# A four-layer transformer kernel: second layer's experts on 23 sorted token spans instead of 72 gated ones

## The reference, cut to what matters

```
logits = x @ Wg                                  # 4096 tokens, 8 experts
probs = softmax(logits)
vals, idx = top_k(probs, 2)
weights = vals / (sum(vals) + 1e-9)
cw = zeros(T, E).at[arange(T)[:, None], idx].set(weights)
act = silu(einsum('th,ehf->tef', x, W1) + b1)     # F = 512
y = einsum('tef,efh->teh', act, W2) + b2
out = einsum('te,teh->th', cw, y)
out = out + 0.1 * (silu(x @ Ws1 + bs1) @ Ws2 + bs2)
```

## Time and profile before

| | us |
|---|---|
| median of 3 runs | 4922.42 |
| the profiled execution, whole | 4929.4 |
| its span, first to last instruction | 4927.6 |
| TensorE busy | 4247.0 (86%) |
| VectorE busy | 3604.9 (73%) |
| ScalarE busy | 3188.9 (65%) |
| GpSimd busy | 2235.6 (45%) |
| granted TensorE clock, mean | 0.942 of full |

### The profile page before, as it was taken

The page is one execution under the profiler, slowest core; times in us unless marked ns, Lnnn a source line. Parts: engine busy times, 40 slices in busy tenths (PEclk is TensorE's granted clock), DMA queues, the critical chain, the costliest instruction groups (busy, mean ns, idle before and its releaser), DMA issues. The chain is left out here.

```text
span 4927.6 us, 91117 instructions
## 1 busy us (share of the span) xinstructions
PE 4247.0 (86%) x35369; PEld 2321.4 (47%) x35370; DVE 3604.9 (73%) x4865; ACT 3188.9 (65%) x4796; POOL 2235.6 (45%) x1299
## 2 busy tenths in 40 slices
PE   5999999999989799677888769995877778999998
PEld 3666666666666444221211124444666343333333
DVE  5888888888845577379888947774776537888887
ACT  2777777777764599347677749992555525555554
POOL 2888888888850133200000003331555435655664
PEclk7999999999999899779999979996999879999999
DMA  2111111111100111300000011110000223334333
GB/s 62 40 40 40 40 40 41 40 39 38 37 12 1 45 65 64 104 25 14 27 18 22 14 45 44 64 43 22 12 12 13 81 81 96 90 92 100 90 96 77
DMA packets 111741, 237.30 MB, mean 48 GB/s; under 512 B 20990, under 2 KB 50942, under 8 KB 108678
## 3 DMA queue, kind: packets, MB, share of 16 engines
q1 hardware_dynamic: 98934, 214.84, 16.1%
q10 hardware_dynamic: 8304, 8.45, 0.6%
q0 software_dynamic: 4096, 8.46, 0.5%
HBM read 161.06 MB, written 28.75 MB: 39 GB/s over the span
## 5 line engine op out<-in xcount | busy, mean ns | idle before, releaser
L528 POOL TENSOR_TENSOR a_prob_low<-a_prob_whole,a_prob_high 128x1024 f16<-128x1024 f32 x512 | 1084.8, 2132 | 276.7 <-ACT a_prob_high L418 272.3
L502 DVE TENSOR_REDUCE a_part_max<-a_top 128x2 f32<-128x1024 f32 x512 | 626.1, 1223 | 218.5 <-PE a_top L329 212.6
L415 ACT ACTIVATE a_prob_whole<-a_score 128x1024 f32<-128x1024 f32 x512 | 525.0, 1025 | 332.5 <-PE a_score L318 320.5
L780 ACT ACTIVATE a_prob<-a_score 128x512 f32<-128x512 f32 x1024 | 532.9, 605 | 259.9 <-PE a_score L724 259.9
L813 DVE TENSOR_REDUCE a_part_max<-a_side 128x2 f32<-128x1024 f32 x512 | 595.1, 1218 | 88.1 <-PE a_side L695 88.1
L2283 DVE TENSOR_TENSOR e_low<-e_whole,e_high 128x512 f16<-128x512 f32 x544 | 453.2, 843 | 168.8 <-ACT e_high L2241 167.4
L1947 POOL TENSOR_TENSOR m_scaled<-m_acted,m_gate 128x512 f32<-128x512 f32 x264 | 402.5, 1531 | 322.3 <-DVE m_acted L2065 245.9
L418 ACT ACTIVATE a_prob_high<-a_score 128x1024 f16<-128x1024 f32 x512 | 522.3, 1020 | 0.0
L317 PE MATMUL a_score<-a_qa,a_ka 128*128 128x256 f16 x2048 | 476.2, 273 | 0.0
L318 PE MATMUL a_score<-a_qb,a_kb 128*128 128x256 f16 x2048 | 476.0, 273 | 0.0
L384 PE MATMUL a_o_ps<-a_v,a_prob_high 128*128 128x65 f16 x4096 | 428.1, 193 | 6.2 <-POOL a_prob_low L528 3.4
(11 more groups left out here) (402 smaller groups left out, 10337.5 us busy)
## 6 DMA issues: line engine op xcount, KB each, us to landing
m_gate<-gates SPq DMA_DIRECT2D x264, 256.0 KB, 5.1
e_gate<-gates SPq DMA_DIRECT2D x17, 2048.0 KB, 7.1
a_ka<-a_nat_high_k SPq DMA_DIRECT2D x128, 128.0 KB, 2.4
e_w<-in_w_moe SPq DMA_DIRECT2D x25, 512.0 KB, 7.8
a_qa<-a_nat_high_q SPq DMA_DIRECT2D x64, 128.0 KB, 2.4
a_qa<-a_nat_low_q SPq DMA_DIRECT2D x64, 128.0 KB, 2.4
a_qb<-a_nat_high_q SPq DMA_DIRECT2D x64, 128.0 KB, 2.4
a_kb<-a_nat_low_k SPq DMA_DIRECT2D x64, 128.0 KB, 2.4
```

The lines of the kernel that those rows point to most:

```text
L415: eng.activation(prob_whole[:, e % RING, :, :, :], score[:, e % 2, :, :, :], ACT.Exp, scale=scale)
L502: eng.tensor_reduce(part_max[:, i, c, :, qt % 4], top[:, :, :], AX.X, ALU.max).then_inc(max_done, 1)
L528: eng.tensor_tensor(prob_low[:, e % RING, :, :, :], prob_whole[:, e % RING, :, :, :], prob_high[:, e % RING, :, :, :], ALU.subtract).then_ ...
L780: eng.activation(prob[:, e % RING, h, :], score[:, step % SLOTS, :], ACT.Exp).then_inc(exp_done, 1)
```

## The change

- A new function `sorted_experts` takes the place of `experts` in e1, and `dispatch` that of `route` in r1. `dispatch` now also sorts: it gives each expert whole spans of 512 slots (its count of pairs rounded up), 23 spans in all (`SORTED = 2 * T // BANK + EXPERTS - 1`), and writes for each span which rows of a DRAM table hold its weights (`w_row`). No pair is dropped. The 8 spans of the shared expert follow behind the 23, on `xn_t` itself.
- r1 now stands ahead of a1. During a1 GpSimd splits the 9 experts' weights into f16 parts and writes them to a table `split_d` (in batch 0), and scatters the 2 x 32 row groups (batches 1 and 2).
- e1's weights are fetched per span by one indirect DMA on GpSimd, 128 rows of 1029 f32 values, into a ring of 4.
- In e1 and e2 the turn and the split of a span are made two spans ahead, with three buffers; e2 has 4 slot buffers instead of 3.
- The clearing of the tables (now three) is cut into 28 DMAs that SyncE issues in a0, one per unit from the third on.
- In a2 the two scatters of a unit stand behind `prod` instead of ahead of it.
- In m3 ScalarE makes Silu of step s ahead of `high` of step s-2, and VectorE makes `lows` of step s-3 instead of s-2.

```diff
+                    if n >= 2:
+                        for to, source in clears[n - 2:n - 1]:
+                            eng.dma_start(to, source).then_inc(cleared, 16)
...
+                    if b == 0:
+                        halves = w_parts[:, 0:8 * P].bitcast(F16)
+                        for e in range(EXPERTS + 1):
+                            if e:
+                                eng.wait_ge(split_out, 16 * e)
+                            eng.dma_start(w_e[:, :], w_moe_d[e, :, :, :].rearrange("p a b -> p (a b)")).then_inc(w_e_in, 16)
+                            eng.dma_start(w_parts[:, 8 * P:W_ROW], b_moe_d[e, :, :]).then_inc(b_e_in, 16)
+                            eng.wait_ge(w_e_in, 16 * (e + 1))
+                            eng.tensor_copy(halves[:, 0:8 * P], w_e[:, :]).then_inc(w_e_high, 1)
+                            eng.wait_ge(w_e_high, e + 1)
+                            eng.tensor_tensor(halves[:, 8 * P:16 * P], w_e[:, :], halves[:, 0:8 * P], ALU.subtract).then_inc(w_e_low, 1)
+                            eng.wait_ge(w_e_low, e + 1)
+                            eng.wait_ge(b_e_in, 16 * (e + 1))
+                            eng.dma_start(split_d[e * P:(e + 1) * P, :], w_parts[:, :]).then_inc(split_out, 16)
+                    elif b < 3:
+                        if b == 1:
+                            eng.wait_ge(cleared, cleared_count)
+                        for t in range(NT):
+                            eng.indirect_dma_start(slots_d, bass.IndirectOffsetOnAxis(slot_of[:, b - 1, t:t + 1], 0),
+                                                   rows[:, b - 1, t, :], None).then_inc(scattered, 16)
...
 linear_attention, GpSimd:
-                    for j in range(2):
-                        eng.indirect_dma_start(slots_d, bass.IndirectOffsetOnAxis(slot_of[:, j, n:n + 1], 0),
-                                               rows[:, j, n, :], None).then_inc(scattered, 16)
...
                     eng.tensor_tensor(prod[:, :, :], q_s[:, r, :, :], k_sum[:, r, :].unsqueeze(1).broadcast_to([P, tiles, P]),
                                       ALU.mult).then_inc(multiplied, 1)
+                    for j in range(2):
+                        eng.indirect_dma_start(slots_d, bass.IndirectOffsetOnAxis(slot_of[:, j, n:n + 1], 0),
+                                               rows[:, j, n, :], None).then_inc(scattered, 16)
...
 mixing_and_experts, VectorE:
-                    s = step_at(slot, HIGH_LAG)
+                    s = step_at(slot, LOW_LAG)
...
 slot_experts:
-    HB, HR, RING = 3, 8, 3
+    HB, HR, RING, XR = 3, 8, 4, 3
...
-                    if span_at(step, 1, -1) >= 0 and step > 0:
-                        turn_in(span_at(step, 1, -1))
+                    if span_at(step, 3, -2) >= 0:
+                        turn_in(span_at(step, 3, -2))
...
-                    if span_at(step, 2, -1) >= 0 and step > 0:
-                        split_x(span_at(step, 2, -1))
+                    if span_at(step, 2, -2) >= 0:
+                        split_x(span_at(step, 2, -2))
...
+def sorted_experts(nc, stage, res_t, xn_t, slots_d, y_d, split_d, w_row, ident_d, filled_sem, filled_count, w_in, sent):
+    J = 4
+    TILES = BANK // P
+    SPANS = SORTED + CH
+    LAG = 4
+    HB, HR, SR, WR, XR = 3, 8, 6, 4, 3
...
+            @block.gpsimd
+            def _(eng):
+                def fetch(s):
+                    if s >= WR:
+                        eng.wait_ge(evacuated, s - WR + 1)
+                    eng.indirect_dma_start(w[:, s % WR, :], None, split_d,
+                                           bass.IndirectOffsetOnAxis(w_row[:, s:s + 1], 0)).then_inc(w_in[s % WR], 16)
+                for s in range(WR):
+                    fetch(s)
+                for step in range(LAST):
+                    s = span_at(step, 0, -2)
+                    if WR <= s <= SORTED:
+                        fetch(s)
+                    s = span_at(step, 3, 2)
+                    if 0 <= s < SORTED:
+                        eng.wait_ge(gated, s + 1)
+                        for t in range(TILES):
+                            eng.indirect_dma_start(y_d, bass.IndirectOffsetOnAxis(dest[:, s, t:t + 1], 0),
+                                                   y_s[:, s % 2, t, :], None).then_inc(sent[s % 2], 16)
...
 program:
-                eng.dma_start(slots_d[0:EXPERTS * CAPACITY, :], d["slots2"]).then_inc(cleared, 16)
-                eng.dma_start(y_d[0:2 * T, :], d["slots2"][:, 0:P]).then_inc(cleared, 16)
-        route(nc, "r1", xn_t, d["w_g1"], None, None, d["ident"], gates[0:EXPERTS + 1, :], EXPERTS,
-              top=2, norm_eps=1e-9, squash="softmax", extra=1, extra_value=0.1, capacity=0)
-        experts(nc, "e1", res_t, xn_t, d["w_moe1"], d["b_moe1"], gates[0:EXPERTS + 1, :],
-                units=EXPERTS + 1, act=ACT.Silu)
```

More of the change, by code:

```diff
@@ L2297, in experts, with dispatch @@
         pl.close()
-def dispatch(nc, stage, xn_t, w_d, tri_d, ident_d, dest_d, base_d, rows, slot_of):
+def dispatch(nc, stage, xn_t, w_d, tri_d, ident_d, dest_d, base_d, rows, slot_of, norm_eps, sort_d, w_row):
     E = EXPERTS
@@ L2435, in _ @@
                 then(eng.tensor_tensor(small[0][:, :].unsqueeze(2), best[:, :, 0:1], best[:, :, 1:2], ALU.add))
+                if norm_eps:
+                    then(eng.tensor_scalar(small[0][:, :], small[0][:, :], norm_eps, None, ALU.add))
                 then(eng.reciprocal(small[1][:, :], small[0][:, :]))
@@ L2512, in slot_experts @@
         gated = pl.sem("gated")
-        sent = [pl.sem(f"sent{r}") for r in range(2)]
         y_loaded = [pl.sem(f"y_loaded{c}") for c in range(CH)]
```

342 lines of the change are left out of this document (298 added, 44 removed).

## The result

The changed kernel took 4779.4 us in the median of 4 runs (4774.93 to 4783.18), beside 4924.4 for the kernel before: a ratio of 0.9705, with a 95% interval of 0.9688 to 0.9721. The prediction was 4680 us and a range from 4630 to 4770. The direction was right, the gain was 145 us instead of 242, and the time lies 9 us outside the range.

The account below looks back on a forecast made before the run. It took TensorE to bound e1, a late token split e2, and VectorE with its waits m3. Terms -14.7 + 4.9 + 2 - 163.0 - 1 - 30.4 - 40 = -242.2 from 4929.4 gave 4687.2, 4680 us median; range 4630 to 4770.

Parts of the forecast that it names:

- the 64 scatters stand behind `low` ..., where GpSimd has nothing else: a1: 64 scatters, 81 us of GpSimd, stand behind `low` of batches 1 and 2 and add nothing to the stage.
- I take 6.5 with the handovers: e1: GpSimd's five indirect DMAs pace 23 sorted spans at 6.5 us each; stage 223.6 for 386.6, gain 163.0 us.
- With the split two spans ahead TensorE stops waiting for it: e2: TensorE no longer waits for the token split; 6.5 us a span, stage 154.4 for 184.8, gain 30.4 us.
- They were hidden before as well, since `prod` started at once: a2: the two scatters, moved behind `prod`, fill GpSimd's 4.46 us wait for `den`; gain 1 us.
- The two bounds are 0 and 99; I take 40: m3: VectorE's 109 us wait for ScalarE's `high` falls away, TensorE is late next; gain 40 us, stage some 838.
- n1 and r1: n1 gains 14.7 us as its constants no longer queue behind clearing DMAs; r1 loses 4.9 us, to 44.8.
- the weight split in a1: a1: splitting 9 experts' weights takes GpSimd 16.8 us each, 151 in all; loss 2 us, from 0 to 20.
- Rival 4: a1: GpSimd's weight split holds `store(1)` up by 30 us, by way of the landings; kernel 4710 us; chance 0.05.
- Rival 3: Indirect DMAs on GpSimd are held up by VectorE, e1 122 us more; kernel 4802 us; chance 0.10.
- Rival 5: e1: a fetch lands through one DMA engine instead of 16, 26 us each; kernel slower, 5146 us; chance 0.04.

Follow-up runs that it names:

- groups 1, 2 and 5: Three groups of runs, each on one chip, of edits against the changed kernel (group 5 with that kernel itself); a1 with its scatters unspaced took 897 to 930 us.
- groups 3 and 4: Two groups of runs, each on one chip, of edits against the changed kernel (group 4 with that kernel itself); a1 with scatters untouched took 835.6 to 839.3 us.
- group 4: The changed kernel once more, unedited, beside three edited kernels on one chip: 4680.6 us, ratio 0.9501 to the kernel before.
- control of group 5: The changed kernel, unedited, beside two edited kernels on one chip: 4803.2 us, with a1 at 927.3 and e1 at 252.2.

## Why the prediction was wrong, step by step

**Where it failed most: "the 64 scatters stand behind `low` ..., where GpSimd has nothing else", cost 0.** I asked what the scatters would delay on their own queue, and found nothing. On the chips of groups 1, 2 and 5, and in the result, a long run of them held up the hand-overs between three engines that have nothing to do with GpSimd: a1 898 to 927 us instead of 839.5. On the chips of groups 3 and 4 it cost nothing and the term was right (835.5 to 839.3). Spreading them, or plain DMAs to neighbouring places instead, takes the loss away on a chip that has it. By what mechanism they hold the others up stays open. No row of the kernel before could have shown it, since nothing runs beside its only long run. But that was the reason to give it a range: "the 64 scatters" was an operation with known duration and unknown neighbours, and it was entered without bounds.

**e1: "I take 6.5 with the handovers", 223.6 us.** Without the delay the step was right: 216.8 us in group 4, and 6.51 us a span once it is steady (2971.86 to 3063.03, 14 spans), with GpSimd's indirect DMAs standing one behind the other as predicted. Over all 22 from first to last it is 6.2, since the first spans are made ahead. With the delay it is 7.4 from first to last, and in the profile of the result 8.3 once steady (3069.04 to 3168.59, 12 spans), which come as one of 14 us and two of 5 to 6. The fetch itself cost GpSimd 0.99 us, as guessed from the scatters, and without it TensorE's 6.05 us a span takes over, as the sum had it. A span with five indirect DMAs leaves GpSimd no pause, and taking the fifth away takes the delay away. That the delay here is the same one as in a1 is inferred from their coming and going together in all groups: in the profile of the result only 5.8 us of e1's waits are put down to "remote", in the control of group 5 it is 36, over VectorE and ScalarE together.

**e2: "With the split two spans ahead TensorE stops waiting for it", 154.4 us.** It stopped waiting for `x_low`, and the stage came out at 186.0 to 188.7 on every chip. What was late next was the low part of the next expert's weights. The pace was right: the 6.5 us that I took are 6.47 once the order is mended, though GpSimd, which never pauses then, needs all of it and not the 6.1 of my sum. What I left out was the order: the split stands behind the four scatters of a span that is done only just before. I wrote that a stall's end must name what is late next, and for e2 named no instruction.

**a2: "They were hidden before as well, since `prod` started at once", gain 1.** The step failed on a reading: `prod` at 3611.69 follows a `q_s` that ended at 3611.59, and I took that for its release. It belongs to another half of the work; GpSimd had come free at 3611.66. The gap shown at `scaled` (4.46 us) was not spare time either: it shrank to 2.48 and the unit with it, from 12.1 us to 10.6, so the gap was part of a loop through several engines, and the wait only says on which engine the loop stands. Undoing the edit gave the 45 us back.

**m3: "The two bounds are 0 and 99; I take 40".** The mechanism was right (the wait for `high` went from 109.1 us in 800 to 5.0 in 780), and the term measured 31.4 us and, undone, 26 to 29. VectorE is now 684 of 780 us busy, and its wait for `acted` grew from 24.6 us to 52.0.

**n1 and r1** came out within 1.3 us each (16.0 gained for 14.7, 6.1 lost for 4.9), the weight split in a1 at no cost.

**The rivals.** Rival 4 (a1 held up by the weight split) named the right stage for the wrong reason. Rival 3 (indirect DMAs slowed by VectorE) did not come: by the Trainium skill (SBUF — State Buffer, SBUF: two separate sides) GpSimd's descriptors are what waits; here the indirect DMAs kept their median of 0.97 us, and in the delay it was VectorE and ScalarE that waited. Rival 5 (a fetch through one DMA engine, 26 us) is excluded by steady spans of 6.5 us with a fetch in each; from SyncE's queue it took 4.7 us from issue to landing. The 3.2 us that the Trainium skill's rule gives for it (DMA: Bandwidth & Descriptors, Anatomy of one DMA) is for a DMA from GpSimd's queue, and when such a fetch landed no trace here shows, so no run tests the rule.

That the changed kernel took 4680.6 us on one chip, the predicted number, is luck and no proof of the sum: there a2 still gave 43 us more than predicted, e2 33 less and m3 12 less, and the errors cancel.

## What to carry to other kernels

A GpSimd indirect DMA is not free because its queue is empty. If many are to go out beside work of other engines, pace them by a count that those engines raise anyway, or move what can be a plain DMA to another queue. A mean of 2 us apart was enough here; runs of eight cost a1 dearly and e2 nothing, so the tolerable run has to be tried in the stage at hand. In a stage where several engines hand work around, a sum per engine isn't enough: write down for the borders, too, in what order the engine that does several jobs takes them, and name the instruction that is late next. Take a rate from the steady part of a stage, since a mean over all spans has the ones made ahead in it. And before a difference of a few per cent is put down to an edit, run the unedited kernel on the same chip.

## What the runs showed of the hardware that I had not expected

- In long runs of indirect DMAs 1.27 us apart the other engines' instructions start 6 to 13 us late on the chip of the result and on those of groups 1, 2 and 5 (a1 898 to 927 us); on those of groups 3 and 4 they don't (836 to 839). The kernel before is alike on all to 0.2%. What it is that piles up was not found: the DMA engines are 14 to 16% busy, plain DMAs from the same queue don't do it, and the profile names "remote". Eight scatters at a time of 128 values a row in e2 did no harm on a chip with the delay, where eight of 130 values in a1 did; it wasn't tried whether the size of the rows, the table they go to or the work beside them makes the difference.
- Where TensorE was held up toward the end of a run of only eight, the clock granted to it fell to 0.50 (1.2 GHz), and it was still there 20 us after the run; this cost more than the hold-up itself: 86 us more of TensorE's busy time for the same matmuls (735.2 against 649.2), of the 90 us that the stage was longer.
- SyncE can fetch a block whose row it reads from SBUF into a register, and the 24 loads of 514.5 KB landed after 4.7 us.
